# Row-maximum score matmuls of two heads in the two 64-row halves of the array, in a cross-attention kernel

## What is computed

```
xn = (input - mean_n) * rsqrt(var_n + EPS) * gamma + beta
q = Wq @ xn + bq ;  k, v = split(Wkv @ context + bkv)          # 64 channels for each head
att = softmax(einsum("nhqc,nhkc->nhqk", q * 64**-0.25, k * 64**-0.25), axis=-1)
y = einsum("nhqk,nhkc->nhqc", att, v)
out = input + Wo @ y + bo
```

## Time and profile before

| | before |
|---|---|
| median of 3 runs | 257.28 us |
| span of the profiled execution | 255.2 us |
| PE busy | 229.4 us (90%) |
| DVE busy | 211.6 us (83%) |
| ACT busy | 203.2 us (80%) |
| POOL busy | 198.5 us (78%) |
| row-maximum matmuls | 256, L399 |
| maxima on DVE | 128, 664 ns each, L733 |

### The profile page before, as it was taken

One profiled execution on the slowest core, in us unless ns is written; L12 is line 12 of the kernel. 1 busy time (PEld: TensorE's weight loads), 2 busy tenths in 40 slices (PEclk: granted clock), 3 DMA queues, 4 the chain that ended last, 5 costly groups with the idle time before them and its releaser, 6 DMA issues.

```text
span 255.2 us, 8140 instructions
## 1 busy us (share of the span) xinstructions
PE 229.4 (90%) x2746; PEld 203.3 (80%) x2746; DVE 211.6 (83%) x446; ACT 203.2 (80%) x391; POOL 198.5 (78%) x188
## 2 busy tenths in 40 slices
PE   0571969999999999999999999999999999999982
PEld 0571747888898889888888898888888889888871
DVE  2399998899988888888888888888888888887875
ACT  2343345999899999999999999999999989998970
POOL 3047968577999797979797979797979888989580
PEclk9999996899999999999999999999999999999997
DMA  6999402010111111112121212121212121010000
GB/s 141 215 293 213 98 0 84 25 52 14 53 44 55 44 55 38 56 31 62 32 62 32 62 32 62 32 62 32 62 32 62 33 64 35 13 32 13 13 4 22
DMA packets 13412, 15.08 MB, mean 59 GB/s; under 512 B 2064, under 2 KB 11920, under 8 KB 13200
## 3 DMA queue, kind: packets, MB, share of 16 engines
q1 hardware_dynamic: 13072, 14.16, 20.9%
q10 hardware_dynamic: 320, 0.66, 1.2%
HBM read 5.90 MB, written 1.05 MB: 27 GB/s over the span
## 4 chain that ended last, share of the span: by engine, by line
PE 71%; DVE 17%; DMA 4%; issue 3%; ACT 2%; POOL 2%; SPq 0%; POOLq 0%
PE ps_sc L380 12%; PE ps_max L399 11%; PE ps_sc L381 10%; PE ps_t L362 7%; PE ps_z L416 6%; PE ps_z L418 5%; PE ps_m L451 5%; PE ps_z L417 5%; PE ps_t L363 5%; DMA x_res<-x_tiles 4%; DVE neg_max L733 4%; PE ps_m L450 4%; DVE t_b L717 3%; DVE x_all L644 2%; DVE x_seq L644 1%
## 5 line engine op out<-in xcount | busy, mean ns | idle before, releaser
L605 POOL TENSOR_TENSOR p_lo<-p_full,p_hi 128x512 f16<-128x512 f32 x122 | 144.9, 1194 | 32.6 <-ACT p_full L525 31.2
L733 DVE TENSOR_REDUCE neg_max<-ps_max 128x2 f32<-128x512 f32 x128 | 84.5, 664 | 0.0
L523 ACT ACTIVATE p_hi<-ps_sc 128x512 f16<-128x512 f32 x128 | 76.1, 595 | 5.0 <-PE ps_sc L381 0.6
L525 ACT ACTIVATE p_full<-ps_sc 128x512 f32<-128x512 f32 x128 | 76.6, 599 | 0.6 <-POOL p_lo L605 0.6
L380 PE MATMUL ps_sc<-t_a,c_seq 128*128 128x256 f32 x256 | 73.0, 306 | 0.0
L381 PE MATMUL ps_sc<-t_b,c_seq 65*128 65x256 f32 x256 | 67.6, 284 | 0.0
L416 PE MATMUL ps_z<-u_hi,p_hi 128*128 128x65 f16 x512 | 60.8, 196 | 1.2 <-POOL p_lo L605 1.0
L417 PE MATMUL ps_z<-u_lo,p_hi 128*128 128x64 f16 x512 | 59.6, 193 | 0.0
L418 PE MATMUL ps_z<-u_hi,p_lo 128*128 128x65 f16 x512 | 59.3, 193 | 0.0
L416 PEld LDWEIGHTS ps_z<-u_hi,p_hi 128*128 128x128 f16 x512 | 45.6, 97 | 7.3 <-DVE z_n L740 0.7
L380 PEld LDWEIGHTS ps_sc<-t_a,c_seq 128*128 128x128 f32 x256 | 49.3, 193 | 0.7 <-issue 0.6
(11 more groups left out here) (100 smaller groups left out, 310.6 us busy)
## 6 DMA issues: line engine op xcount, KB each, us to landing
ctx_raw<-ctx SPq DMA_DIRECT2D x8, 256.0 KB, 16.4
c_seq<-c_all SPq DMA_DIRECT2D x16, 128.0 KB, 2.0
x_seq<-x_all SPq DMA_DIRECT2D x14, 128.0 KB, 2.0
c_max<-c_all SPq DMA_DIRECT2D x14, 128.0 KB, 2.0
x_res<-x_tiles SPq DMA_DIRECT2D x4, 256.0 KB, 7.1
z_n<-ctx_flat SPq DMA_DIRECT2D x1, 1024.0 KB, 13.6
c_seq<-c_all SPq DMA_DIRECT2D x16, 64.0 KB, 2.0
out<-x_res SPq DMA_DIRECT2D x16, 64.0 KB, 1.7
```

The costliest lines, as they stand in the source:

```text
L523: nc.scalar.activation(p_hi[:, buf, :, :].rearrange("p t s -> p (t s)"), scores, ACT.Exp).then_inc(act_phi, 1)
L525: nc.scalar.activation(p_full[:, head % 2, :], scores, ACT.Exp).then_inc(act_p, 1)
L605: nc.gpsimd.tensor_tensor(p_lo[:, buf, :, :].rearrange("p t s -> p (t s)"), p_full[:, head % 2, :], p_hi[:, buf, :, :].rearrange("p t s -> ...
L733: nc.vector.tensor_reduce(neg_max[:, (par + dn) % 2, head, :], ps_max[:, head % 2, :].rearrange("p (t s) -> p t s", t=KT), X, ALU.max, neg ...
```

## The change

The row-maximum matmuls of a pair of heads (head, head + 1) are issued together in the even step, four of them: for each half qt of the queries one with the first head on partitions 0 to 63 and one with the second on partitions 64 to 127, into bank 0 and bank 1 of `ps_max`. Both use the rounded context alone, so `c_max` now holds it on both halves of the partitions: for sequences 0 and 1 a POOL instruction writes it, for the others SP issues two DMAs of 64 rows. The pair waits for both maxima of the pair before. DVE takes both maxima in the odd step. The remainder of the context takes no part in the row maximum any more; any number near the maximum serves there, since it cancels in the softmax.

```diff
@@ block.sync, step
-                    sp.dma_start(c_max_to[:, q:q + 1, :], c_from[:, bass.ds(m, 1), :]).then_inc(dma_cmax[q], 16)
+                    for rows in (slice(0, C), slice(C, P)):
+                        sp.dma_start(c_max_to[rows, q:q + 1, :], c_from[0:C, bass.ds(m, 1), :]).then_inc(dma_cmax[q], 16)
@@ block.tensor, step
-                if e := at(n, h, MAX_AHEAD):
-                    m, dn, head = e
-                    q, bank = (par + dn) % 2, head % 2
-                    if direct(m):
-                        c_m = c_all[:, m, :]
-                        need(pe, pool_c_lo, 1)
-                    else:
-                        c_m = c_max[:, q, :]
-                        if head == 0:
-                            need(pe, dma_cmax[q], 16 * (fills(half, par, dn) - 1))
-                    if head % 2 == 0:
-                        need(pe, act_thi, m * PAIRS + head // 2 + 1)
-                    need(pe, dve_max, m * H + head - 1)
+                if h % 2 == 0 and (e := at(n, h, MAX_AHEAD)):
+                    m, dn, head = e
+                    q = (par + dn) % 2
+                    if head == 0:
+                        if direct(m):
+                            need(pe, pool_cmax, 1)
+                        else:
+                            need(pe, dma_cmax[q], 32 * (fills(half, par, dn) - 1))
+                    need(pe, act_thi, m * PAIRS + head // 2 + 1)
+                    need(pe, dve_max, m * H + head)
                     for qt in range(KT):
-                        last = mm(ps_max[:, bank, qt * S:(qt + 1) * S], t_a[:, q, head, qt * P:(qt + 1) * P], c_m,
-                                  start=True, stop=True)
-                    last.then_inc(pe_s1, 1)
+                        for k in range(2):
+                            rows = slice(k * C, (k + 1) * C)
+                            last = mm(ps_max[:, k, qt * S:(qt + 1) * S], t_a[rows, q, head + k, qt * P:(qt + 1) * P],
+                                      c_max[rows, q, :], start=True, stop=True)
+                            if qt == KT - 1:
+                                last.then_inc(pe_s1, 1)
@@ block.gpsimd
+            pool.wait_ge(dma_c[0], 32)
+            nc.gpsimd.tensor_scalar(c_max[:], ctx_raw[:, 0:DIRECT, :], 1.0, 1.0, ALU.mult, ALU.mult).then_inc(pool_cmax, 1)
             split_ctx(0)
@@ block.vector, step
-                if e := at(n, h, MAX_AHEAD):
-                    m, dn, head = e
-                    need(dve, pe_s1, m * H + head + 1)
-                    nc.vector.tensor_reduce(neg_max[:, (par + dn) % 2, head, :],
-                                            ps_max[:, head % 2, :].rearrange("p (t s) -> p t s", t=KT), X, ALU.max,
-                                            negate=True).then_inc(dve_max, 1)
+                if h % 2 == 1 and (e := at(n, h - 1, MAX_AHEAD)):
+                    m, dn, head = e
+                    for k in range(2):
+                        need(dve, pe_s1, m * H + head + k + 1)
+                        nc.vector.tensor_reduce(neg_max[:, (par + dn) % 2, head + k, :],
+                                                ps_max[:, k, :].rearrange("p (t s) -> p t s", t=KT), X, ALU.max,
+                                                negate=True).then_inc(dve_max, 1)
```

More of the change, by code:

```diff
@@ L134, in xattn_program @@
         dve_plo, dve_z1 = sem("dve_plo"), sem("dve_z1")
-        pool_xn, dve_ones = sem("pool_xn"), sem("dve_ones")
+        pool_xn, dve_ones, pool_cmax = sem("pool_xn"), sem("dve_ones"), sem("pool_cmax")
         pool_c_hi, pool_c_lo, pool_xb = sem("pool_c_hi"), sem("pool_c_lo"), sem("pool_xb")
```

## The result

| | before | after |
|---|---|---|
| median (4 runs each, taken together) | 257.74 us | 271.29 us |
| ratio | | 1.0485 [1.0403, 1.0567] |
| span of the profiled execution | 255.2 us | 269.7 us |
| 60 to 220 us: PE, DVE, ACT busy | 159.5, 137.0, 145.9 | 158.1, 149.1, 138.2 |

The kernel is slower by 13.5 us; +6.2 was forecast. Some executions of every kernel here fall into a second, slower state; the ratios and their intervals compare fast runs alone, the medians take all runs. The page after, engine shares of the chain that ended last, then PE, DVE and granted clock in 40 slices of 6.7 us; PE's share of the chain falls from 71 to 56%, and in its fifth and seventh slice it is at 6 and 8, where the earlier trace rows has 9 and 9.

A forecast was written before the change was run, and what follows sets the result against it. PE's order was taken to bound the loop, DVE the start-up. Span 255.2 us, +5.0 for 56 pairs, +1.0 start-up = 261.2; with the median 2.1 above span 263.3, stated as 263.5; 8-in-10 range 257 to 277.

The forecast's parts named there:

- I take full overlap: Row-maximum matmuls on PE: the two row halves run side by side, saving 0.25 us for a pair.
- Going in: 0.20: PE, between L381 and a pair's four matmuls: the change from 128-row to 64-row mode costs 0.20 us.
- +0.09 us for a pair: PE in the loop: two mode changes, 0.34 us, against 0.25 saved; 56 pairs give +5.0 us.
- Going out ... 0.13: PE, from a pair's four matmuls to L416: the change back to 128-row mode costs 0.13 us.
- the start-up, +1: Until 50 us, where DVE has the say: PE's waits between maxima add +0.3 to +2 us, taken as +1.
- three or four: Start-up hand-overs from DVE's maxima to PE, each leaving 0.2 us, or 0.6 if the halves don't overlap.
- The rest costs nothing: POOL's 0.62 us context copy and SP's extra DMA for each sequence: hidden in idle time, zero cost.
- the slack is only 0.1 to 0.3: DVE's maxima to PE's next pair in the loop: 0.1 to 0.3 us of slack, so no wait.
- (b): Rival: the row halves don't overlap because their weight loads go one after the other; 277 us, chance 0.18.
- (c): Rival: DVE's hand-over late by 0.3 us in two pairs of a sequence, 8.4 us more; 272 us, chance 0.12.
- (d): Rival: the mode change is mostly hidden or shorter, at half price 0.17 us; 254 to 257 us, chance 0.12.
- (e): Rival: no cost for mode changes and the halves overlap, so faster; about 250 us, chance 0.08.

The follow-up runs named there:

- one_half: The changed kernel with both heads' row-maximum matmuls on rows 0 to 63, so the two can't run side by side; 288.21 us.
- after_busy: The changed kernel with 36 matmuls, whose result nobody reads, added in PE's start-up waits; 263.52 us, ratio 1.0195.
- before_busy: The kernel before the change with 29 matmuls, whose result nobody reads, added in PE's start-up waits; 256.42 us, ratio 0.9974.
- order128: The changed order alone, with full-height 128-row matmuls on the stacked context, without POOL's copy and the second context DMA; 268.44 us, ratio 1.0419.

## Why the prediction was right and wrong

**Right: the direction, and the mechanism in the loop.** "I take full overlap" held: 3 to 4 ns from half to half, and 0.23 us lost for a pair in one_half (0.25 said). "Going in: 0.20" held: 0.094 more ahead of the first matmul and 0.10 more behind it. No matmul waits for DVE in the steady loop of the profile (five weight loads do, 0.8 us in all from 88 to 214 us), and PE is busy for 99%.

**Mis-sized: +0.09 us for a pair.** It is +0.045, since "Going out ... 0.13" is 0.086 (0.208 in place of 0.122): 0.20 + 0.086 - 0.244 = 0.04. 56 pairs are 2.5 us, not 5.0. In the last sequences a half sequence has 6.70 us, 0.08 more again: at three of the five pairs in the trace from 215 to 230 us L382 to L399 is 0.26 to 0.32 us instead of 0.21 (215.38 to 215.64, 225.02 to 225.34), with the maximum ended 0.15 us ahead.

**Wrong: the start-up, +1.** This is the step that failed: up to the 7th mark the profile lost 11.4 us. The forecast counted "three or four" hand-overs at up to 0.6 us each. These were sized about right: some 1.4 of the 2.8 us up to the 1st mark in after_busy against before_busy. What it left out is what a wait does to the matmuls behind it: 7.8 us by after_busy, of which the kernel before had lost 0.9 too, and so about half of all that the change costs. The row was there to be read: the earlier trace rows shows two matmuls taking 0.77 us where the earlier trace rows has 0.40. I had used the slow rhythm as the price of one pair and not asked when it ends and what puts that off. And "The rest costs nothing" put POOL's copy at zero, where some 1.4 us go with it: POOL had the idle time, as forecast, but DVE, which "has the say" there, got its work done later.

**Wrong: of DVE, "the slack is only 0.1 to 0.3".** In the steady loop one pair in four has none: the maxima's record ends at 132.30 and PE enters at 132.35. With full-height matmuls (order128) one pair in two is held, at 0.18 us. Between the 4th and the 7th mark, where DVE is full, the zero should have been 1.6 us. The working also took z's add at its old 0.41 us; it takes 1.41.

**Rivals.** (b) fell by one_half. (c), DVE's hand-over late, is what happened in the start-up and in two periods after it, but not in the loop, where it had its price of 8.4. (d) is about a third true: the changes cost 0.28 for a pair, between the 0.34 of the forecast and the 0.17 of (d), and the sign turns below 0.25. (e) fell by the entry of 0.21. The range (257 to 277) held the result; the likeliest case's own, 260.5 to 267, did not. That the wide range held is luck. Two opposite errors met in it: from the 7th to the 31st mark, 48 pairs, 1.3 us too much (4.3 forecast, 3.0 measured), and 9.7 too little ahead of it (1.7 and 11.4).

## What to carry to other kernels

Packing half-height matmuls side by side gives back one stream of two and pays two changes of row mode, here 0.24 against 0.28 us; put them beside other half-height work, and look whether what they need of the order (both results awaited together) fits a start-up in which the other engine has the say. A wait of one or two microseconds on PE may not be paid once: ask at which rhythm the matmuls behind it run, and until when; a few idle matmuls inside the wait were worth 7.8 us here. When instructions of DVE and POOL that read SBUF move against each other, look up who now starts inside whom: here one such add cost DVE 1.0 us a sequence, and the kernel 0.25 once PE was quicker. That goes for a small instruction added to the start-up too.

## What the hardware showed

- Two matmuls in different 64-row halves start 3 to 4 ns apart. The Trainium skill, TensorEngine Tiling (Array Packing), Tiling Modes, has tiles working in parallel and a change of mode draining the array. Both agree with the trace, in which the change costs 0.19 us going in (half ahead of the first matmul, half behind it) and 0.09 going out.
- DVE's operations on two SBUF operands, started within a POOL instruction, lasted until that one had ended: the add 1.41 us for 0.41 (to 0.28 us past POOL's end), a subtraction of 32 columns 1.06 us, one on a single element 1.95 us. Where DVE's add and POOL's subtraction started together, POOL's took longer instead, 1.45 for 1.16 us. DVE's maxima and `t_b`, which read PSUM, were not held (0.66 to 0.68 us in both kernels). The Trainium skill, Trainium Architecture — The Big Picture, section What this means for kernel authors, says that the port pair of these two engines is an exclusive lock and not a split of bandwidth; the trace agrees.
- The column of the granted clock reads 1.00 where the trace holds no record of the clock. Of two kernels with like waits the windows of 33 to 46 us are, first order128, then after:

```profile
33.00:46.00 13.00, 11.06 (x42) 9.10 (x42) 10.20 (x18) 5.28 (x10) 8.94 (x7) 0.50 0.14 41
```

```profile
33.00:46.00 13.00, 9.40 (x37) 6.49 (x37) 10.94 (x18) 4.56 (x9) 8.14 (x7) 1.00 0.16 42
```

Matmuls are 0.213 us apart in both. In order128 the clock had come up at 28.1 us and fallen at 31.5, so there are records. The trace of after has its first one at 64.1 us, where the clock comes up; ahead of it the column, and the page's `PEclk` line, say 1.00 all through the slow stretch. Up to the first record the distance from start to start has to be read. Why 64-row matmuls come with a later rise (63 to 67 against 49 and 51 us) isn't shown by any run beyond that they do.
